# Masked attention in a decoder kernel: one VectorE pass marks the dead places, GpSimd normalises before its small work, inputs are copied ahead of the exponentials, and two small operations change engine in the sister stages

## What is computed

```python
q = decoder_output @ wq_w + wq_b            # 16 heads of 8 features
k = encoder_output @ wk_w + wk_b
v = encoder_output @ wv_w + wv_b
score = einsum('bhqd,bhkd->bhqk', q, k) / sqrt(8)
score = score * mask
score = where(score == 0, -1e9, score)
alignment = softmax(score, axis=-1)
context = einsum('bhqk,bhkd->bhqd', alignment, v)
heads = context @ wo_w + wo_b               # then layernorm(x + heads)
```

## Time and profile before

| | us |
|---|---|
| median of 3 runs (7273.56 to 7288.13) | 7275.91 |
| the profiled execution, its own time | 7289.72 |
| its span | 7288.1 |
| stage f0, about | 3245 to 3602 |
| stage x1, about | 5440 to 5995 |
| stage ea, about | 6064 to 6825 |

### The profile page before, as it was taken

The page is one execution under the profiler, slowest core; times in us unless marked ns, Lnnn a source line. Parts: engine busy times, 40 slices in busy tenths (PEclk is TensorE's granted clock), DMA queues, the critical chain, the costliest instruction groups (busy, mean ns, idle before and its releaser), DMA issues. The chain is left out here.

```text
span 7288.1 us, 153320 instructions
## 1 busy us (share of the span) xinstructions
PE 5388.3 (74%) x51100; PEld 3084.5 (42%) x51100; DVE 5588.1 (77%) x10280; ACT 3409.9 (47%) x4719; POOL 3046.5 (42%) x2540
## 2 busy tenths in 40 slices
PE   4777777777777775868688888798866556888790
PEld 1222222222222233546555555566654445666440
DVE  3999999999999975879755555566659875999544
ACT  3555565555565542546422222244434433666450
POOL 5333334433334233656400000354448864777443
PEclk8888888888888787989899999799887777999895
DMA  1111111111111122211100000000000111222343
GB/s 39 43 38 44 44 37 44 39 44 43 38 43 40 38 72 52 54 39 38 50 14 13 13 13 11 27 17 18 17 20 26 28 43 48 71 71 71 97 146 96
DMA packets 567491, 317.20 MB, mean 44 GB/s; under 512 B 60697, under 2 KB 557532, under 8 KB 566556
## 3 DMA queue, kind: packets, MB, share of 16 engines
q1 hardware_dynamic: 556700, 304.49, 15.1%
q10 hardware_dynamic: 7680, 3.15, 0.2%
q0 software_dynamic: 2560, 2.63, 0.1%
HBM read 169.59 MB, written 52.43 MB: 30 GB/s over the span
## 5 line engine op out<-in xcount | busy, mean ns | idle before, releaser
L1331 ACT ACTIVATE mb_dA<-ps,mb_a_neg 128x1024 f32<-128x1024 f32 x1008 | 1122.5, 1114 | 771.7 <-PE ps L1101 678.2
L1675 DVE TENSOR_TENSOR mb_m<-mb_dA,ps 128x512 f32<-128x512 f32 x2016 | 1282.9, 675 | 30.5 <-PE ps L1116 18.5
L1683 DVE TENSOR_TENSOR ps<-mb_m,ps 128x512 f32<-128x512 f32 x1984 | 1271.2, 684 | 40.7 <-PE ps L1116 40.7
L1116 PE MATMUL ps<-mb_ur,mb_bl 64*128 64x256 bf16 x4032 | 450.5, 307 | 505.1 <-DVE mb_m L1675 498.2
L1128 PE MATMUL ps<-mb_m,mb_cz 128*32 128x256 f32 x8064 | 741.9, 444 | 3.6 <-DVE mb_m L1675 2.4
L1116 PEld LDWEIGHTS ps<-mb_ur,mb_bl 64*128 64x128 bf16 x4032 | 122.0, 98 | 1050.3 <-DVE mb_m L1675 983.9
L1101 PE MATMUL ps<-mb_ur,mb_sel 64*128 64x256 bf16 x4032 | 453.2, 309 | 121.6 <-ACT mb_dA L1331 95.2
L2368 DVE TENSOR_TENSOR mo_gu<-mo_gate,ps 128x512 f32<-128x512 f32 x288 | 195.5, 684 | 364.6 <-ACT mo_gate L2288 364.6
L2228 PE MATMUL ps<-mo_hT,mo_wg 128*128 128x512 f32 x576 | 317.4, 634 | 139.9 <-DVE mo_gu L2368 139.9
L2288 ACT ACTIVATE mo_gate<-ps 128x512 f32<-128x512 f32 x288 | 170.3, 597 | 534.2 <-PE ps L2229 534.0
L1101 PEld LDWEIGHTS ps<-mb_ur,mb_sel 64*128 64x128 bf16 x4032 | 154.3, 102 | 416.1 <-ACT mb_dA L1331 263.1
(11 more groups left out here) (451 smaller groups left out, 13380.0 us busy)
## 6 DMA issues: line engine op xcount, KB each, us to landing
mb_ur<-mb_pc SPq DMA_DIRECT2D x768, 64.0 KB
mb_bl<-mb_pc SPq DMA_DIRECT2D x576, 64.0 KB
ef_w<-in_ef_w SPq DMA_DIRECT2D x35, 514.5 KB
ea_wqk<-in_ea_wqk SPq DMA_DIRECT2D x70, 129.0 KB
ea_wvo<-in_ea_wvo SPq DMA_DIRECT2D x70, 128.5 KB, 2.1
ea_x<-hidden SPq DMA_DIRECT2D x280, 32.0 KB, 2.0
ea_ln_rows<-in_ea_ln SPq DMA_DIRECT2D x70, 128.0 KB, 3.1
pairs<-ea_y SPq DMA_DIRECT2D x70, 128.0 KB, 2.5
```

Source lines behind the costliest of these rows:

```text
L1116: mm = nc.tensor.matmul(ps[:, UB + 2 * (t % 2) + g, 256 * pl:256 * pl + 256], bl[k, j % 2, tl, 128 * pl:128 * pl + 128], ur[k, j % 2, tl], ...
L1331: nc.scalar.activation(dA[:, t % RING].rearrange("p (g n) -> p g n", g=2), ps[:, DT:DT + 2, :], ACT.Exp, scale=a_neg[:, 0:1]).then_inc(dA_ ...
L1675: nc.vector.tensor_tensor(m[:, t % RING, half], dA[:, t % RING, half], ps[:, UB + 2 * ((t - 1) % 2) + g, :], ALU.mult).then_inc(m_ready.se ...
L1683: nc.vector.tensor_tensor(u, m[:, t % RING, 512 * g:512 * g + 512], u, ALU.add).then_inc(h_ready.sem, 1)
```

## The change

In the masked stage x1:

- DVE marks dead places in one pass of its own. After the two mask products it computes `(p == 0) - p` in place (`scalar_tensor_tensor`), takes the row minimum instead of the maximum, and the exponential gets the scale -1e9 instead of 8^-0.5; the queries are made smaller by SCALE/GONE in `take_qk` so that the values come out alike. The `dead` tile and POOL's `add_dead` go away.
- The keys are spread over the heads by ACT: `take_qk` writes `km` with four activations that read PSUM and use the head mask as a scale, and one more writes the queries. POOL's `mask_heads` goes away.
- The order on POOL becomes `normalise(j)`, `tail_scale(j-2)`, `add_bias(j+2)`.
- The order on DVE becomes `mask_scores(j+1)`, `sums(j)`, `finish(j-2)`, `softmax_shift(j+1)`.
- On ACT, `take_x(j+3)` comes before `exponentials(j)`.

In stage f0, `norm(j+4)` moves from DVE to ACT, behind `take_x(j+3)`; `norm_scale` waits for it. In stage ea, `affine(j-3)` moves from DVE to POOL, to the head of its period. PE's instructions and SP's are the same in all stages but for the semaphores waited on.

```diff
@@ PE, scores @@
-                    pe.wait_ge(km_ready.sem, km_ready.at(i))
+                    if mask is None:
+                        pe.wait_ge(km_ready.sem, km_ready.at(i))
@@ ACT @@
+                def norm(i, u):
+
+                    act.wait_ge(nrstd_ready.sem, nrstd_ready.at(i))
+                    act.wait_ge(xT_done.sem, xT_done.at(i - 1))
+                    for t in range(2):
+                        nc.scalar.activation(xn[:, t], x[:, u, t], ACT.Identity, scale=nrstd[:, t:t + 1]).then_inc(
+                            xn_ready.sem, 1)
...
-                    if qkv_bias:
+                    if mask is not None:
+                        for n in range(4):
+                            ins = nc.scalar.activation(
+                                km[:, u % 2, :, n, :], lead_ps[:, 256:512].rearrange("p (b k) -> p b k", b=4), ACT.Identity,
+                                scale=head_mask[:, n:n + 1], bias=bkm[:, n:n + 1])
+                        ins.then_inc(qk_taken.sem, 1)
+                        nc.scalar.activation(qT[:, u % 2], lead_ps[:, 0:256], ACT.Identity, scale=SCALE / GONE,
+                                             bias=bkm[:, 4:5]).then_inc(qk_taken.sem, 1)
+                    elif qkv_bias:
...
                 def period(j, u):
                     two, three, past = (u + 2) % 4, (u + 3) % 4, (u - 1) % 4
+                    if mask is not None and live(j + 3):
+                        take_x(j + 3, three)
                     if live(j):
                         exponentials(j, u)
-                    if live(j + 3):
+                    if mask is None and live(j + 3):
                         take_x(j + 3, three)
+                    if pre_norm and live(j + 4):
+                        norm(j + 4, u)
@@ POOL @@
-                    pool.wait_ge(normed.sem, normed.at(i, 4))
+                    pool.wait_ge(normed.sem, normed.at(i))
+                    pool.wait_ge(xn_ready.sem, xn_ready.at(i - 1))
...
-                def add_dead(i, u):
-                    pool.wait_ge(dead_ready.sem, dead_ready.at(i))
-                    nc.gpsimd.tensor_tensor(p[:, u], p[:, u], dead[:], ALU.add).then_inc(s_masked.sem, 1)
+                def affine(i, u):
...
                 def period(j, u):
                     two = (u + 2) % 4
-                    if live(j + 2):
+                    if tail == "affine" and live(j - 3):
+                        affine(j - 3, (u - 3) % 4)
+                    if mask is None and live(j + 2):
                         mask_heads(j + 2, two)
-                    if mask is not None and live(j + 1):
-                        add_dead(j + 1, (u + 1) % 4)
+                    if mask is not None and live(j):
+                        normalise(j, u)
                     if tail != "none" and live(j - 2):
                         tail_scale(j - 2)
                     if pre_norm and live(j + 5):
                         norm_scale(j + 5)
                     if qkv_bias and live(j + 2):
                         add_bias(j + 2, two)
-                    if live(j):
+                    if mask is None and live(j):
                         normalise(j, u)
@@ DVE @@
                     dve.wait_ge(masked.sem, masked.at(i))
-                    dve.wait_ge(s_masked.sem, s_masked.at(i - 1))
-                    nc.vector.tensor_scalar(dead[:], p[:, u], 0.0, -1e9 / SCALE, ALU.is_equal, ALU.mult).then_inc(
-                        dead_ready.sem, 1)
+
+                    nc.vector.scalar_tensor_tensor(p[:, u], p[:, u], 0.0, p[:, u], ALU.is_equal, ALU.subtract).then_inc(
+                        s_masked.sem, 1)
...
-                    if pre_norm and live(j + 4):
-                        norm(j + 4, u)
                     if pre_norm and live(j + 5):
                         square_means(j + 5, one)
-                    if tail == "affine" and live(j - 3):
-                        affine(j - 3, past)
                     if mask is not None and live(j + 1):
                         mask_scores(j + 1, one)
-                    if not rope and live(j - 2):
+                    if not rope and mask is None and live(j - 2):
                         finish(j - 2, two)
                     if live(j):
                         sums(j, u)
+                    if mask is not None and live(j - 2):
+                        finish(j - 2, two)
```

More of the change, by code:

```diff
@@ L133, in attention8 @@
     SCALE = 8.0 ** -0.5
+    GONE = 1e9
     has_ctx = ctx is not None
@@ L206, in attention8 @@
             mk = st.sb("mk", [128, 4, 2, 64])
-            dead = st.sb("dead", [128, 2048])
+            bkm = st.sb("bkm", [128, 5])
         if plan:
@@ L222, in attention8 @@
         y_stored = st.slot_signal("y_stored", 1, slots=4)
-        consts_set = st.counter("consts_set", 1 + 2 * causal)
+        consts_set = st.counter("consts_set", 1 + 2 * causal + 2 * (mask is not None))
         half_set = st.counter("half_set", 3 + pre_norm)
-        normed = st.counter("normed", 6)
+        normed = st.counter("normed", 4)
+        xn_ready = st.counter("xn_ready", 2)
         nrstd_ready = st.counter("nrstd_ready", 2)
@@ L314, in lead @@
                     if pre_norm:
-                        sp.wait_ge(normed.sem, normed.at(i - 4))
+                        sp.wait_ge(xn_ready.sem, xn_ready.at(i - 4))
                     else:
@@ L550, in take_qk @@
                     act.wait_ge(qk_done.sem, qk_done.at(i))
-                    act.wait_ge(km_ready.sem, km_ready.at(i - 1))
+                    if mask is None:
+                        act.wait_ge(km_ready.sem, km_ready.at(i - 1))
                     act.wait_ge(s_done.sem, s_done.at(i - 2))
-                    if qkv_bias:
+                    if mask is not None:
[7 more added lines that the diff above has]
+                    elif qkv_bias:
                         nc.scalar.activation(kT[:], lead_ps[:, 256:512], ACT.Identity, bias=wqk[:, slot(u), 257:258]).then_inc(
@@ L574, in exponentials @@
                     act.wait_ge(shifted.sem, shifted.at(i))
-                    nc.scalar.activation(p[:, u], p[:, u], ACT.Exp, scale=SCALE).then_inc(exp_done.sem, 1)
+                    nc.scalar.activation(p[:, u], p[:, u], ACT.Exp, scale=SCALE if mask is None else -GONE).then_inc(
+                        exp_done.sem, 1)
                 def take_p(i, t):
@@ L696, in _ @@
                         period(4 * r + u, u)
-                for j in range(HI, LAST + 1):
+                for j in range(HI, LAST + 2):
                     period(j, j % 4)
@@ L704, in set_constants @@
                     nc.vector.memset(vbd[:], 0.0).then_inc(consts_set.sem, 1)
+                    if mask is not None:
+                        dve.wait_ge(w_loaded.sem, w_loaded.at(0))
+                        nc.vector.tensor_scalar(bkm[:, 0:4], head_mask[:], wqk[:, 0, 257:258], None, ALU.mult).then_inc(
+                            consts_set.sem, 1)
+                        nc.vector.tensor_scalar(bkm[:, 4:5], wqk[:, 0, 256:257], SCALE / GONE, None, ALU.mult).then_inc(
+                            consts_set.sem, 1)
                     if causal:
@@ L712, in square_means @@
                     dve.wait_ge(x_loaded.of(u), x_loaded.at(i, u))
+                    dve.wait_ge(nrstd_ready.sem, nrstd_ready.at(i - 1))
                     for t in range(2):
@@ L724, in square_means @@
                     nc.vector.tensor_tensor(nsq[:], nsq[:], nmv[:, :, 1], ALU.add).then_inc(normed.sem, 1)
[L726 to L733, removed]
                 def times_cos(i, u):
@@ L782, in softmax_shift @@
                         src = S_ps.rearrange("p g (c k) -> p (g c) k", k=64)
-                    nc.vector.reduce_max(top[:], src, AX.X).then_inc(top_ready.sem, 1)
+                    if mask is not None:
+                        nc.vector.tensor_reduce(top[:], src, AX.X, ALU.min).then_inc(top_ready.sem, 1)
+                    else:
+                        nc.vector.reduce_max(top[:], src, AX.X).then_inc(top_ready.sem, 1)
                     dve.wait_ge(top_ready.sem, top_ready.at(i))
@@ L818, in finish @@
                         nc.vector.bn_aggr(mv[:, t], stats[:, t]).then_inc(tailed.sem, 1)
[L820 to L829, removed]
                 def period(j, u):
-                    one, two, three, past = (u + 1) % 4, (u + 2) % 4, (u + 3) % 4, (u - 3) % 4
+                    one, two, three = (u + 1) % 4, (u + 2) % 4, (u + 3) % 4
                     if rope and live(j + 2):
                         add_turned(j + 2, two)
-                    if pre_norm and live(j + 4):
-                        norm(j + 4, u)
                     if pre_norm and live(j + 5):
                         square_means(j + 5, one)
-                    if tail == "affine" and live(j - 3):
-                        affine(j - 3, past)
                     if mask is not None and live(j + 1):
                         mask_scores(j + 1, one)
-                    if not rope and live(j - 2):
```

(3 more changed lines are left out.)

11 lines of the change are left out of this document (9 added, 2 removed).

## The result

The changed kernel takes 7376.53 us (median, 7361.94 to 7384.32) against 7274.81 before: a ratio of 1.0134, 95% interval 1.0118 to 1.0149. It is slower by 102 us, and 7378 was forecast. Its profiled execution took 7384.32 us with a span of 7382.4, 94 us more than the span before. Both kernels' medians lie under their profiled executions, by 15 us before and 8 after, so stage sums are compared between the spans.

What follows compares the result with a forecast made beforehand. It took a chain of waits across DVE, POOL, ACT and PE, not only DVE's load, to set x1's period. Terms: x1 +143, f0 -21, ea -20, sum +102, so 7378 against the 7275.9 median; range 7300 to 7410.

Steps and rivals of the forecast that it cites:

- The chain that bounds x1: x1: waits over DVE, POOL, ACT and PE set the period, 16.34 us before and 21.36 after, 5.02 more.
- the link: x1: PE's next scores wait through ACT's scale for tail_scale, behind normalise on POOL; j = 2 to 29, 28 x 5.02 = +140.6.
- the PE part: x1: from the start of PE's values to DVE's next mask products, priced at 4.91 us.
- +143: x1: forecast change of the whole stage in us, slower, including its start and end.
- Who goes first at the port: x1: DVE's waiting subtraction goes before POOL's tail_scale, putting 2.15 us in the chain.
- Start and end of x1: x1: intervals before the first tail take 13.22 by DVE alone, the one before them -3; last two tails +8.
- SP's steps: ea: SP can do a quad every 9.96 us, so 62 steps with a fetch give -9.
- DVE's 1.45: ea: DVE loses at least 1.45 us; by DVE and the round, period about 9.2, stage 60 us shorter.
- POOL's port: ea: by the skill's shared-port warning the move would give nothing, total 20 higher; no meeting was expected.
- the input's lead: ea: compute may come closer to SP's fetches of x, with 5.5 us in hand, once.
- the tail chain: x1: the chain through normalise, the subtraction, tail_scale, scale and PE to the next mask products, 21.36 us.
- rival B: x1: link through ACT's scale is off the path, DVE's list alone sets 13.22 a quad, total 7144; chance 0.12.

Runs made afterwards that it cites:

- the half subtraction: The changed kernel with x1's subtraction of the row minimum covering only the first half of the columns; 7352.12 us, ratio 1.0094.
- e7_merged_fetches: The changed kernel with two DMAs a quad fewer on SP in ea, their rows travelling in two tables fetched anyway; 7327.03 us, ratio 1.0062.
- e1_pool_order: The changed kernel with POOL in x1 running tail_scale and add_bias ahead of normalise again, DVE's order staying new; 7236.93 us, ratio 0.9932.
- e8_residual_split: The changed kernel with, in x1, scale last on ACT, mask load before store on SP, and DVE's finish split in two; 7164.04 us, ratio 0.9833.

## Why the prediction was right

- *The chain that bounds x1.* It closed before at 16.34 and was to close at 21.36; the 28 intervals in which the link exists took 21.06 on average (5473.3, reckoned from the rows of the first three, to 6062.92), for a mean of 16.39 before. The extra was 4.67 a quad where the prediction had 5.02. The steps new to the chain came out as priced (marking 2.29 for 2.32, `sums` to reciprocal 2.38 for 2.36, reciprocal to `normalise` 0.43, the subtraction 2.15 behind `normalise`), and `tail_scale` to `scale` took 1.33 for 1.40. The term that was too large is the PE part: 4.91 fits the mean before (4.90), but after the change it took 4.71 on average, between 4.18 and 5.26. The prediction had expected a lower granted clock at most to lengthen it; the clock fell, and PE's part was shorter all the same. 28 x 0.35 = 10 us is what x1 is under the +143: +133.
- *The link itself.* Shown three ways: by putting POOL's order back, by putting DVE's back alone, which makes it worse, and by moving `scale`.
- *Who goes first at the port.* Taken from one meeting in the earlier trace rows and used for another pair of instructions; the half subtraction confirmed it. The Trainium skill, "SBUF — State Buffer", section "Who interferes with whom", says that issue order decides who blocks, and the trace agrees: the subtraction was issued at 5674.00 and the tail's operation, which then took 2.25, at 5674.31.
- *Start and end of x1.* The two intervals without a tail that were priced took 13.10 and 13.09 for 13.22, the one before them lost 3.5 for 3, and the end cost +9 for +8.
- *f0.* 9.20 for 9.18, -21 for -21. The last periods of the stage before had shown the next bound.
- *ea.* -19 for -20, and for the reason given: SP's steps, not DVE's 1.45 or POOL's port. The first 62 intervals gave 15 (9 were priced for SP's steps and 5.5 for the input's lead, used up once; PE now waits for the input), the last seven gave 4 for 6. The warning of the Trainium skill, "Perfetto Trace Analysis", section "Optimizing Scalar/DVE Operations", that moving work between DVE and GpSimd might not help, did not come true here: the moved operations ran mostly beside DVE's subtraction, which in ea reads PSUM for one input, and all 140 of them took 0.72 to 0.74 us. `e7_merged_fetches` agrees, since ea fell at once to 9.21 with `affine` still on POOL.
- *What was missed.* Two things that cost nothing here and would have in a variant. Moving `finish` behind `sums` makes PE's first `values` wait for the residual sum, 6 us a period; the tail chain hid it. And the mask's load behind the store on SP, which bound only once `scale` had moved: the prediction's rival B put 7144 on x1 without the link through ACT, but cutting only that link gives 7290, because two more rings (chains that close on themselves) lie just beneath it, through the mask's load (18.12) and through the residual sum (15.69). The rival was priced by DVE's list alone, and that was too cheap.

## What to carry to other kernels

When queues run in order, ask of each reordering not what is computed earlier but what now stands behind what: follow the waits over the engines until the chain comes back to its own start one period later, and add it up. If the sum before equals the measured period, as 16.34 did here, the sum after is worth trusting (21.36 for a measured 21.06); if a ring is cut, expect the next one close beneath and look for it (in f0 the last periods of the stage showed it uncut). A change that makes all of an engine's work shorter can lose if it puts a long operation of another engine ahead of a short one that somebody waits for.

## What the runs showed of the hardware

- A GpSimd operation on two columns took 2.25 us instead of 0.20 behind a VectorE subtraction with two SBUF inputs that had been issued 0.31 earlier, and 1.18 when that subtraction was half as long. `scalar_tensor_tensor` with both inputs the same SBUF tile took 2.29 for 2048 columns, about the 2.32 of the subtraction running free.
- What such a meeting costs depends on how much of the other instruction is left: in `e1_pool_order` `normalise` came 0.08 us ahead of the subtraction and cost it 3.4 us; in `e8_residual_split` it came 2.8 ahead and cost 0.7.
- The mean granted clock of a stretch does not tell what one group of matmuls gets. The 32 matmuls of `scores` took 1.12 us in each of 25 periods of `e1_pool_order`, at a mean clock of 0.78 in 5500 to 5900, and 1.78 on average (1.12 to 2.01) in the kernel before, at a mean of 0.80.
- SP's step with nine DMAs and five looked-up values takes 9.96 us on average in the changed kernel, more than the 9.21 in which the engines can do a quad of 256 tokens. With two DMAs fewer its own work is some 8.85, although as many bytes reach SBUF.
